# The third stream takes two chunks of experts per step, their outputs first, and DVE weighs both in the step between

## The reference

```python
probs = jax.nn.softmax(xf @ router_w + router_b, axis=-1)      # 64 experts
tw, ti = jax.lax.top_k(probs, K)                               # K = 8
tw = tw / jnp.sum(tw, axis=-1, keepdims=True)
def body(acc, p):
    W1, B1, W2, B2, e = p
    h = jax.nn.silu(xf @ W1 + B1) @ W2 + B2
    cw = jnp.sum(jnp.where(ti == e, tw, 0.0), axis=-1)
    return (acc + cw[:, None] * h, None)
routed, _ = jax.lax.scan(body, jnp.zeros_like(xf), (w1, b1, w2, b2, jnp.arange(w1.shape[0])))
shared = jnp.sum(jax.vmap(shared_mlp)(sw1, sb1, sw2, sb2), axis=0)   # silu(xf @ W1 + B1) @ W2 + B2
x = x + jnp.tanh(g_ffn[1]) * (routed + shared)
```

## Time and profile before

| | us |
|---|---|
| median of 3 runs (lowest, highest) | 886.76 (885.13, 886.98) |
| the profiled execution, device time | 885.65 |
| its span, first to last instruction | 883.9 |
| busy in the span: PE, DVE, ACT, POOL | 723.4, 569.2, 533.9, 304.5 |

### The profile page before, as it was taken

The page is one execution under the profiler, slowest core; times in us unless marked ns, Lnnn a source line. Parts: engine busy times, 40 slices in busy tenths (PEclk is TensorE's granted clock), DMA queues, the critical chain, the costliest instruction groups (busy, mean ns, idle before and its releaser), DMA issues.

```text
span 883.9 us, 15786 instructions
## 1 busy us (share of the span) xinstructions
PE 723.4 (82%) x5368; PEld 472.7 (53%) x5368; DVE 569.2 (64%) x2212; ACT 533.9 (60%) x1345; POOL 304.5 (34%) x296
## 2 busy tenths in 40 slices
PE   5758788897878775788869789869887898889997
PEld 3436465564556654554546465546564664675443
DVE  5676856778657748648867757647566575873623
ACT  3348495775827336355596695795785845544442
POOL 4254524455421233223445324335233124312200
PEclk9888999998987978789999999999899898879999
DMA  8610010101100000202121301200202001004252
GB/s 260 193 29 15 14 43 13 39 6 22 34 13 1 2 1 1 82 2 68 36 67 37 90 14 45 75 1 22 69 26 56 18 26 30 13 13 125 73 129 91
DMA packets 37162, 41.83 MB, mean 47 GB/s; under 512 B 14345, under 2 KB 23771, under 8 KB 36955
## 3 DMA queue, kind: packets, MB, share of 16 engines
q1 hardware_dynamic: 37083, 40.83, 16.8%
HBM read 28.75 MB, written 2.62 MB: 35 GB/s over the span
## 4 chain that ended last, share of the span: by engine, by line
PE 45%; DVE 26%; ACT 17%; POOL 6%; issue 3%; DMA 1%; SPq 1%; DVEq 0%; POOLq 0%; ACTq 0%
ACT work L855 8%; PE act_psum L606 5%; PE moe_psum L616 5%; PE dve_psum L438 4%; PE act_psum L499 3%; PE dve_psum L509 3%; DVE work L1122 3%; DVE stats L1091 2%; DVE res_nrm L1100 2%; PE act_psum L705 2%; PE act_psum L768 2%; PE dve_psum L708 2%; PE dve_psum L715 2%; POOL work L1509 2%; PE act_psum L425 2%
## 5 line engine op out<-in xcount | busy, mean ns | idle before, releaser
L1509 POOL TENSOR_TENSOR work<-work,rinv 128x512 f32<-128x512 f32 (+1 forms) x72 | 77.6, 1085 | 147.2 <-DVE rinv L1108 146.8
L855 ACT ACTIVATE work<-work,nbias,rnorm 128x128 f32<-128x128 f32 x256 | 122.6, 481 | 7.9 <-DVE nbias L1185 7.5
L1491 POOL TENSOR_SCALAR rstd<-mv 128x4 f32<-128x4 f32 x36 | 10.0, 277 | 173.0 <-DVE mv L1094 172.8
L1549 POOL TENSOR_TENSOR hT<-hT,work 128x512 f32<-128x512 f32 x32 | 40.7, 1271 | 77.9 <-DVE work L1145 77.9
L438 PE MATMUL dve_psum<-wqkv,hTs 128*128 128x512 f32 x128 | 66.0, 640 | 1.5 <-ACT hTs L1002 1.3
L838 ACT COPY v_loc<-act_psum 77x512 f32<-77x512 f32 (+2 forms) x72 | 41.5, 582 | 36.0 <-PE act_psum L443 16.6
L1122 DVE CUSTOM_DVE_ANT_0 work<-dve_psum,masks 128x128 f32<-128x128 f32 x256 | 58.3, 282 | 3.3 <-PE dve_psum L469 3.3
L425 PE MATMUL act_psum<-ident,res_nrm 128*128 128x128 f32 x96 | 25.3, 363 | 41.9 <-DVE res_nrm L1100 41.9
L838 ACT COPY hT<-act_psum 128x512 f32<-128x512 f32 (+1 forms) x60 | 31.1, 523 | 43.7 <-PE act_psum L499 22.4
L953 ACT ACTIVATE work<-act_psum,cols 128x512 f32<-128x512 f32 x40 | 27.4, 687 | 36.3 <-PE act_psum L606 36.2
L1555 POOL TENSOR_TENSOR v_loc<-v_loc,rnorm 128x512 f32<-128x512 f32 x32 | 33.3, 1062 | 46.0 <-DVE rnorm L1164 46.0
(11 more groups left out here) (224 smaller groups left out, 2015.3 us busy)
## 6 DMA issues: line engine op xcount, KB each, us to landing
ahead<-cwT_dram SPq DMA_DIRECT2D x128, 64.0 KB, 2.0
v_loc<-v_loc SPq DMA_DIRECT2D x24, 256.0 KB, 3.7
kT<-cwT_dram SPq DMA_DIRECT2D x80, 64.0 KB, 2.1
qT<-cwT_dram SPq DMA_DIRECT2D x48, 64.0 KB, 2.0
wqkv<-in_wqkv_dram SPq DMA_DIRECT2D x2, 768.0 KB
res_nrm<-in_x_dram SPq DMA_DIRECT2D x4, 256.0 KB, 3.1
w_m<-in_w_m_dram SPq DMA_DIRECT2D x1, 1024.0 KB, 8.7
v_loc<-v_loc SPq DMA_DIRECT2D x8, 128.0 KB, 3.2
```

The costliest lines, as they stand in the source:

```text
L855: last = nc.scalar.activation(weights[:, i, :], weights[:, i, :], ACT.Exp, bias=nbias[u][:, b, i:i + 1], scale=scale_of(i), accum_out=sums ...
L1509: nc.gpsimd.tensor_tensor(some, some, by.unsqueeze(2).to_broadcast(list(some.shape)), ALU.mult).then_inc(ready[u], 1)
L1549: nc.gpsimd.tensor_tensor(own, own, partners[u][:, t % 2, k, :], ALU.add).then_inc(turned_ready[u], 1)
```

## The change

The third stream's loop goes in strides of two. In an even step PE does the outputs of the two chunks before, then the hidden products of two new chunks, and ACT takes both with silu, one right behind the other. In the odd step between, PE and ACT have nothing of this stream; DVE weighs both chunks, and SP refills both tiles `ahead`. Two tiles `units` take turns instead of three (the third is used for the sum alone). The number of steps is the same, and so is each product, silu, weighing and DMA. The bias rows are added in the same step as the last two outputs. `TURNS` is not changed.

```diff
--- before.py
+++ after.py
@@ -619,14 +619,18 @@
 
                     yield
                     pe.wait_ge(experts_in_loaded, 16 * (u + 1))
-                    for c in range(CHUNKS + 2):
-                        if c < CHUNKS:
-                            expert_hidden(u, c, experts_in)
-                        if c >= 2:
-                            expert_out(u, c - 2, units[(c - 2) % 3][:])
-                        if c == CHUNKS + 1:
+                    for c in range(0, CHUNKS + 2, 2):
+
+                        for k in (c - 2, c - 1):
+                            if c >= 2:
+                                expert_out(u, k, units[k % 2][:])
+                        for k in (c, c + 1):
+                            if c < CHUNKS:
+                                expert_hidden(u, k, experts_in)
+                        if c == CHUNKS:
                             pe.wait_ge(ahead_ready[0], ahead_fills(u, ROUTED))
                             nc.tensor.matmul(moe_psum[:], b_m2[:], ahead[0][0:EXPERTS, :], start=False, stop=True).then_inc(moe_filled, 1)
+                        yield
                         yield
                     pe.wait_ge(moe_emptied, u + 1)
                     bank = dve_bank(("moe_out", u))
@@ -962,13 +966,15 @@
 
                 def deferred_experts(u):
                     yield
-                    for c in range(CHUNKS + 2):
-                        if c < CHUNKS:
-                            bank = filled(("moe_h", u, c))
-                            bias = col("sb1", c) if c < SHARED else col("moe_b1", c - SHARED)
-                            nc.scalar.activation(units[c % 3][:], bank[:], ACT.Silu, bias=bias).then_inc(act_emptied, 1)
-                        if c == CHUNKS + 1:
+                    for c in range(0, CHUNKS + 2, 2):
+                        for k in (c, c + 1):
+                            if c < CHUNKS:
+                                bank = filled(("moe_h", u, k))
+                                bias = col("sb1", k) if k < SHARED else col("moe_b1", k - SHARED)
+                                nc.scalar.activation(units[k % 2][:], bank[:], ACT.Silu, bias=bias).then_inc(act_emptied, 1)
+                        if c == CHUNKS:
                             expert_sum(u, units[2][:])
+                        yield
                         yield
                     yield
                     yield
@@ -1294,13 +1300,14 @@
 
                 def deferred_experts(u):
                     yield
-                    for c in range(CHUNKS + 2):
-                        k = c - 1 - SHARED
-                        if 0 <= k < ROUTED:
-                            rows_of, weights = units[(c - 1) % 3][:], ahead[k % AHEAD][:]
-                            dve.wait_ge(ahead_ready[k % AHEAD], ahead_fills(u, k))
-                            dve.wait_ge(act_emptied, act_item["moe_h", u, c - 1] + 1)
-                            nc.vector.tensor_tensor(rows_of, weights, rows_of, ALU.mult).then_inc(weighed_ready[u], 1)
+                    for c in range(0, CHUNKS + 2, 2):
+                        yield
+                        for k in (c - SHARED, c - SHARED + 1):
+                            if 0 <= k < ROUTED:
+                                rows_of, weights = units[k % 2][:], ahead[k % AHEAD][:]
+                                dve.wait_ge(ahead_ready[k % AHEAD], ahead_fills(u, k))
+                                dve.wait_ge(act_emptied, act_item["moe_h", u, k + SHARED] + 1)
+                                nc.vector.tensor_tensor(rows_of, weights, rows_of, ALU.mult).then_inc(weighed_ready[u], 1)
                         yield
                     bank = filled(("moe_out", u))
                     dve.wait_ge(ahead_ready[1], ahead_fills(u, ROUTED))
@@ -1662,17 +1669,18 @@
                         sp.wait_ge(x_stored[u - 1], 16)
                     fill_ahead(1)
                     yield
-                    for c in range(CHUNKS + 2):
-                        k = c - 1 - SHARED
-                        if 0 <= k < ROUTED:
-                            sp.wait_ge(weighed_ready[u], k + 1)
-                            if k + AHEAD < ROUTED:
-                                fill_ahead(k + AHEAD)
-                            elif k + AHEAD == ROUTED:
-                                sp.dma_start(ahead[0][0:EXPERTS, :], cwT_dram[u]).then_inc(ahead_ready[0], 16)
-                            else:
-                                sp.wait_ge(x_kept[u], 16)
-                                sp.dma_start(ahead[1][:], x_dram[u]).then_inc(ahead_ready[1], 16)
+                    for c in range(0, CHUNKS + 2, 2):
+                        yield
+                        for k in (c - SHARED, c - SHARED + 1):
+                            if 0 <= k < ROUTED:
+                                sp.wait_ge(weighed_ready[u], k + 1)
+                                if k + AHEAD < ROUTED:
+                                    fill_ahead(k + AHEAD)
+                                elif k + AHEAD == ROUTED:
+                                    sp.dma_start(ahead[0][0:EXPERTS, :], cwT_dram[u]).then_inc(ahead_ready[0], 16)
+                                else:
+                                    sp.wait_ge(x_kept[u], 16)
+                                    sp.dma_start(ahead[1][:], x_dram[u]).then_inc(ahead_ready[1], 16)
                         yield
                     yield
                     sp.wait_ge(dve_emptied, dve_item["moe_out", u] + 1)
```

## The result

| | before | after |
|---|---|---|
| median of 4 runs, us | 885.94 (884.08 to 886.98) | 897.86 (894.93 to 900.17) |
| ratio to before | | 1.0141, 95% [1.0115, 1.0167] |
| profiled execution, us | 885.65 | 900.17 |
| span, us | 883.9 | 898.4 |
| TensorE clock, mean | 0.902 | 0.903 |

The change makes the kernel about 12 us slower; 880.8 us and "faster" were forecast. The profiled execution is the longest of the four, 2.3 us above the median. In the changed kernel 859 is the exponential (855 before), 974 the silu (969), 1310 the weighing (1303); 606 and 616 kept their numbers.

What follows compares the result with a forecast made beforehand. No engine was taken to bound the whole; ACT's exponentials bound four stretches, PE and DVE in turn the rest. Loads -7.7 and one PE pair +1.7 gave -6.0 us, so 880.8 us, range 875.5 to 888.5.

Steps and rivals of the forecast that it cites:

- Table loads: On ACT: eleven of 56 table loads vanish, six of them on the chain at 1.283 us each, 7.7 us gained.
- The four blocks: ACT-bound exponentials of samples 2 and 3's local attention; each stretch was to become 1.3 to 2.6 us shorter.
- PE, four products at a time: On PE: third-stream products grouped in fours leave some gaps bare; cost taken as one pair, 1.7 us.
- my bounds of 0 to 18: Cost of PE's grouped products: nothing if gaps merge, at most half of the 37 us hidden in gaps, 18 us.
- the twelve on the norm: PE's twelve waits on the norm, 16.0 us, said to be there in spite of the filling; reason for a low cost.
- At nothing; if that cover fails: On DVE: two weighings in a row cost nothing, since PE asks one third-stream step later; otherwise 0.68 us per double step.
- The third, cover lost: Rival: bare turns between double steps leave PE waiting and the clock falls; eight lost pairs, 13.8 us, 892.8 us; chance 0.15.
- Its clock part: On PE: after a long wait the granted clock falls to 0.50, so a lost pair costs 3.4 us instead of 1.72.
- The fourth rival: On ACT: a table switch costs more than its load, 2.66 us; six switches give 870.8 or 872.5 us; chance 0.03.
- rival 2: ACT is freed but PE, POOL and DVE take over the pace or a bare gap eats the gain; about 886 us; chance 0.14.
- sample 3's feed-forward: Sign for the forecast: it starts about 2 us earlier after sample 2's first exponentials.
- the signs against me: PE's waits between 376 and 766 us growing over 8 us, mean clock falling, or outputs waiting for DVE's weighing.

Runs made afterwards that it cites:

- s2: Changed kernel with the outputs moved to the odd step, a fourth units tile, and DVE weighing and SP refilling one tile per step; 876.48 us.
- s2r: s2 with relu in place of silu in the third stream, 20 table loads; 865.63 us.
- rb: Kernel before with relu in place of silu in the third stream, 20 table loads instead of 56; 866.88 us.
- s3: Changed kernel with three units tiles, one output and both hidden products in the even step, other output in the odd, one weighing a step; 878.33 us.
- hf: Changed kernel with the hidden products ahead of the outputs in the double step, using a fourth units tile; 893.58 us.
- s1: Changed kernel with the outputs moved to the odd step, a fourth units tile, both weighings still in the odd step; 882.59 us.
- det2: det with one weighing and one refill per step instead of two together; 887.25 us.
- det: Changed kernel where DVE multiplies the weights tile by itself and PE's outputs don't wait for it; 892.29 us.
- bd: Kernel before with weighings and refills in pairs every second step, outputs one step later, a fourth units tile; 883.7 us.
- ra: Changed kernel with relu in place of silu in the third stream, 20 table loads instead of 45; 883.77 us.
- b31: Kernel before with only the outputs in pairs every second step, so three and one products on PE, a fourth units tile; 886.92 us.

## Why the prediction was wrong

- *Table loads, 7.7 us of gain.* Right, as mechanism and as size where the order lets it come through: s2 8.7 us, with s2r and rb, the same two orders without these loads, 1.3 us apart, less than their intervals. In after only about 5 us of it, with a wide interval. The four blocks should have become shorter by 1.3, 1.3, 2.6 and 1.3 us, 6.4 in all; in after 2.3, 0.6, 1.0 and -0.8 came, 3.1 in all. In s3, with the same loads, it was 2.9, 1.4, 1.1 and 1.4, 6.8 in all. The count of loads on the chain was thus about right in sum and not place by place, and in after half of it is missing.
- *The step that failed: "PE, four products at a time ... I take one pair, 1.7 us, near the lower end".* By itself it is 11.0 us (hf against s1; 10.8 by det2 against s2), inside my bounds of 0 to 18 and nowhere near 1.7. Table loads at 7.7 against a clump at 11 would already have turned the forecast into "slower". The reason I gave, "the twelve on the norm were there in spite of the filling", was read the wrong way round: those waits were what was left over behind the filling. The earlier trace rows gives what the filling did not hide, and says nothing of what it hid. The other number was at hand: 37 of 70.5 us were hidden. With every second step empty, half of that, my upper bound of 18 us, says how many products may come to lie bare, and that fits: 21 us more in after's chain, 20.8 in det2's against s2. In time about half of it was paid. An estimate between the bounds, 9 us, would have been near; I took the lower end for a reason that the earlier trace rows does not give.
- *DVE, "At nothing; if that cover fails, 0.68 us at each of the 20 double steps".* The cover failed seven times, 8.0 us, a mean of 1.1 us, and it costs 5.6 us by det, 4.3 by hf. The weighings stand one third-stream step ahead in the lists, but in time DVE is only just at them: in the place shown above PE asks at 429.60 us, and DVE had begun the first of the two at 428.94; one weighing can take 1.7 us. (There are 16 such pairs, not 20: the shared chunks are not weighed. And 18 of the double steps have four products; the first and the last of each sample have two.) Two weighings in a row are another 5 us in these steps (det2); in bd they are nothing, so this term hangs on the place.
- *The rivals.* The third, cover lost, 892.8 us, was the case, at 0.15; it named eight bare pairs, 13.8 us; the size fits (11.0 and 5.6), the count of pairs was not looked for. Its clock part is the smaller one: the mean clock of the kernel is 0.903 (0.902 before), that of the stretch 0.90 (0.92). PE is busy 7.2 us longer in it; with 45% of the span on the chain, as PE has in the earlier trace rows, that is an estimated 3 us. det, with PE busy for 723.6 us in all as before (723.4), is 6.9 us slower than before, so most of the loss needs no clock, and hf against s1 has its 11.0 us, and ra against rb its 16.9, without a lower clock in the mean. In the first stretch, where the loss arises, the products shown behind a wait do run at a granted clock of 0.50, in the kernel before as well. No run took the clock alone. The Trainium skill (TensorE: Matmul & The Clock Gate, HAM oscillation) has work in bursts with waits between pay in clock. It pointed the right way, slower; by the runs here most of the price is waiting that the burst no longer covers. The fourth rival is refuted: the earlier trace rows has 6.0% of 390 us, 23 us or 18 loads, on the chain; rb, which takes 36 of the 44 loads of that stretch away, gained 18.3 us. ACT is busy 46.3 us less in it, 1.29 for each of 36. At the 2.66 us that the Trainium skill has for a load and its drain (ScalarE: Activation LUTs, What ACT_TABLE_LOAD costs), the 18 would have given an estimated 48 us. (In rival 2's argument the fourth stretch has ACT at 95%, not "96% and more".)
- *The balance.* -8.7 (s2) + 10.8 (clump) + 5.0 (weighings in pairs) + 5.6 (PE's wait for them) = +12.7 us; +11.9 was measured, the rest is the different medians of before (885.22 and 885.94). It closes by construction, since each term is the step from one kernel to the next, and in another order of steps the terms would be others. It holds for this offset alone (shifted by a step, after comes out 5.8 us lower and s3 10.8 us higher).
- *What I said would show it.* 13 and 16 loads and 14 us less of ACT came true. So did sample 3's feed-forward: it starts 4.09 us after sample 2's first exponentials there (702.00 and 706.09 us), 6.09 before (681.22 and 687.31), 2.0 us earlier. Of the signs against me the weighing came (8.0 us), PE's waits grew by 7.8 us where I had put 8, and the stretches outside the four blocks grew by 15.8 us (10.6 of it ahead of the first), more than the 14.0 us that ACT lost. Bare work in the chain, the largest sign, I had not named.

Still open: which double steps ahead of the first two blocks make after's loss, why paired weighings cost 5 us in the odd steps, what part of the clump's price is the clock, and why the offset that gives after 5.8 us costs s3 10.8.

## What to carry to other kernels

Filler work in an in-order queue is worth what it covers: before moving it, sum up how much of it lies off the chain, not how much waiting is left; the price of clumping is a share of the former (here 11 us of 37 hidden). A batching that one engine profits from (ACT's tables) can be kept while the other engine's share is spread by depth (a third tile, outputs one step later); s3 kept the eleven loads that way and took 7.1 us, at this offset. And try the offset of a periodic filler as a size of its own: for s3 one step decided more than the edit did.

## What the hardware showed unexpectedly

- A table load costs 1.283 us on ACT but 0.51 us of the kernel on average when 36 were taken away (18.3 us), and 0.56 us when 25 were taken from after (14.1 us, ra).
- One weighing of 128x512 on DVE took from 657 to 1748 ns; the pair at 428.94 took 3.24 us where POOL ran its 1.27 and 1.72 us products at the same time. That POOL's work slows it is suggested by this timeline and was not tried apart.
- Two of four products right behind a wait took 3.42 us (404.26 in after) at a granted clock of 0.50, the later two 2.51 at 0.67; the pair at 395.70 in the kernel before, at 1.00, took 1.72.
- Of the program more than of the chip: at the unshifted offset three and one products instead of two and two cost 1.5 us (b31, interval 0.2 to 4.5) or 1.9 (s3 against s2), four and none 11. A step later s3 lost all of its gain, so the small price of three and one is not general.
